# LoRA and low-rank residual kernel: half of z made as z^T for two tiles at once

## What is computed

```python
base   = x @ W.T                                      # W: 1024 x 1024
logits = x @ Wr.T + 5.0 * one_hot(itok)               # 8 experts
gates  = softmax over the two largest logits, 0 for the other six
h      = x @ A[e].T for each expert e                 # rank 16 each, 128 columns in all
cond   = base + 2.0 * sum_e gates[e] * h[e] @ B[e].T
out    = x + ((cond @ V) * S) @ U.T                   # V: 1024 x 256, U: 1024 x 256
```

## Time and profile before

| | us |
|---|---|
| median of three runs (lowest, highest) | 156.6 (156.23, 157.12) |
| the profiled execution | 156.3 |
| its span | 154.5 |
| PE busy | 150.1 (97%) |
| VectorE busy | 102.7 (66%) |
| GpSimd busy | 69.9 (45%) |
| ScalarE busy | 65.6 (42%) |
| granted TensorE clock, mean | 1.00 of full speed |

### The profile page before, as it was taken

One profiled execution on the slowest core, in us unless ns is written; L12 is line 12 of the kernel. 1 busy time (PEld: TensorE's weight loads), 2 busy tenths in 40 slices (PEclk: granted clock), 3 DMA queues, 4 the chain that ended last, 5 costly groups with the idle time before them and its releaser, 6 DMA issues.

```text
span 154.5 us, 2555 instructions
## 1 busy us (share of the span) xinstructions
PE 150.1 (97%) x883; PEld 139.9 (91%) x883; DVE 102.7 (66%) x299; ACT 65.6 (42%) x147; POOL 69.9 (45%) x53
## 2 busy tenths in 40 slices
PE   7999999999999999999999999999999999999991
PEld 5899999999988999989998999899999989998880
DVE  0887882942757898684669386929692967386862
ACT  4867772639615532551165125414431642233200
POOL 2000500259556650359355926591669068701800
PEclk9999999999999999999999999999999999999999
DMA  5999999994312064346338645764680087006184
GB/s 176 387 405 406 398 414 408 407 407 154 127 39 97 20 256 136 128 140 275 140 135 305 241 136 208 236 239 136 271 258 18 0 296 249 2 22 251 70 329 148
DMA packets 10669, 32.72 MB, mean 212 GB/s; under 512 B 1440, under 2 KB 1952, under 8 KB 10528
## 3 DMA queue, kind: packets, MB, share of 16 engines
q1 hardware_dynamic: 10368, 31.96, 55.7%
q10 hardware_dynamic: 288, 0.59, 1.0%
HBM read 24.16 MB, written 8.39 MB: 211 GB/s over the span
## 4 chain that ended last, share of the span: by engine, by line
PE 94%; DMA 3%; DVE 1%; ACT 0%; SPq 0%; issue 0%; DVEq 0%
PE pj L322 16%; PE pj L324 16%; PE pj L323 16%; PE fin L322 14%; PE fin L324 13%; PE fin L323 13%; DMA w_raw<-in_W 3%; PE zt L392 2%; PE gt L374 1%; PE zt L322 1%; PE zt L324 1%; PE zt L323 1%; DVE w_lo L704 0%; ACT w_hi L561 0%; DVE x_all L833 0%; SPq L217 0%
## 5 line engine op out<-in xcount | busy, mean ns | idle before, releaser
L278 POOL TENSOR_TENSOR xT_lo<-xt_raw,xT_hi 128x1024 fp32r<-128x1024 f32 x16 | 40.3, 2520 | 54.9 <-ACT xT_hi L576 54.9
L322 PE MATMUL pj<-proj_hi,xT_hi 128*128 128x392 f32 x128 | 45.0, 352 | 0.0
L324 PE MATMUL pj<-proj_hi,xT_lo 128*128 128x392 f32 x128 | 43.6, 341 | 0.0
L323 PE MATMUL pj<-proj_lo,xT_hi 128*128 128x392 f32 x128 | 43.5, 340 | 0.0
L293 POOL TENSOR_TENSOR x_all<-x_all,vw_raw 128x512 f32<-128x512 f32 x18 | 23.0, 1294 | 17.6 <-DVE vw_raw L808 17.6
L322 PE MATMUL fin<-v_hi,w_hi 128*128 128x256 f32 (+1 forms) x84 | 26.9, 320 | 0.1
L324 PE MATMUL fin<-v_hi,w_lo 128*128 128x256 f32 (+1 forms) x84 | 26.4, 314 | 0.0
L323 PE MATMUL fin<-v_lo,w_hi 128*128 128x256 f32 (+1 forms) x84 | 26.4, 314 | 0.0
L322 PEld LDWEIGHTS pj<-proj_hi,xT_hi 128*128 128x128 f32 x128 | 24.1, 188 | 1.0
L323 PEld LDWEIGHTS pj<-proj_lo,xT_hi 128*128 128x128 f32 x128 | 24.1, 188 | 0.5
L324 PEld LDWEIGHTS pj<-proj_hi,xT_lo 128*128 128x128 f32 x128 | 24.0, 188 | 0.0
(11 more groups left out here) (87 smaller groups left out, 230.6 us busy)
## 6 DMA issues: line engine op xcount, KB each, us to landing
xt_raw<-in_xt SPq DMA_DIRECT2D x16, 512.0 KB, 4.0
x_all<-in_x SPq DMA_DIRECT2D x16, 512.0 KB, 5.2
out<-x_all SPq DMA_DIRECT2D x13, 512.0 KB, 3.1
vw_raw<-in_VW SPq DMA_DIRECT2D x6, 384.0 KB, 6.7
w_raw<-in_W SPq DMA_DIRECT2D x8, 256.0 KB, 5.8
out<-x_all SPq DMA_DIRECT2D x5, 256.0 KB, 2.1
u_raw<-in_U SPq DMA_DIRECT2D x1, 1024.0 KB, 14.1
aw_raw<-in_AW SPq DMA_DIRECT2D x1, 544.0 KB, 6.8
```

The costliest lines, as they stand in the source:

```text
L278: nc.gpsimd.tensor_sub(xT_lo[:, t % 2, :, :], xt_raw[:, t % XTR, :, :], xT_hi[:, t % 2, :, :].bitcast(F32)).then_inc(xt_lo, 1)
L322: nc.tensor.matmul(dst, l_hi, r_hi, start=first, stop=False, skip_group_check=shared)
L323: nc.tensor.matmul(dst, l_hi, r_lo, start=False, stop=False, skip_group_check=shared)
L324: return nc.tensor.matmul(dst, l_lo, r_hi, start=False, stop=last, skip_group_check=shared)
```

## The change

The last 128 columns of z are no longer projected with the tile. `project` takes 264 columns (h, logits and the first half of z). `half_t` makes the second half for a pair, as z^T at once: `proj`'s last 128 columns are the stationary operand, x^T of two tiles (256 columns) the moving one. It needs x^T of both tiles, so the rings of split x^T hold four. The first half is copied (`copy_z`, now before the LoRA part is in it) and transposed once a tile, inside `half_t`. `transpose_gh` and `mix` work on a pair: `mix` adds the LoRA part to z^T, with B^T V stationary. `zt` is now ordered by half and tile (`zt_v`), and B^T V moves to the bank `gt`. `b_raw` and `u_raw` share memory with `w_raw`, so that their loads wait until the first 4 and 12 half chunks of W are split.

All lists are written by pair. PE's is: project the even tile, `second_part` of two pairs back, project the odd tile, `first_part` of the pair before, gh transposes, `half_t`, `mix`.

```diff
-        xT_hi = sb("xT_hi", [P, 2, DC, P], F32R)
+        xT_hi = sb("xT_hi", [P, XTR, DC, P], F32R)
...
# SP
                 if k == 6:
-                    sp.dma_start(b_raw[:, :, :], B).then_inc(b_load, 16)
-            load_xt(1)
+                    sp.wait_ge(w_lo_done, 4)
+                    sp.dma_start(b_raw, B).then_inc(b_load, 16)
+            for t in range(1, XTR):
+                load_xt(t)
             sp.dma_start(s_col[:, :], S).then_inc(s_load, 16)
-            sp.dma_start(u_raw[:, :, :], U).then_inc(u_load, 16)
-            for t in range(2, XTR):
-                load_xt(t)
+            sp.wait_ge(w_lo_done, 12)
+            sp.dma_start(u_raw, U).then_inc(u_load, 16)
             for t in range(XR):
                 load_x(t)
...
+            for p in range(PAIRS):
+                if 2 * p >= XR:
+                    load_x(2 * p)
+                    load_x(2 * p + 1)
+                if 2 * p + XTR < TILES:
+                    load_xt(2 * p + XTR)
+                    load_xt(2 * p + 1 + XTR)
+                if p == 2:
+                    store_head(0)
+                    store_head(1)
+                if p >= 3:
+                    store_pair(p - 2)
...
# GpSimd
             split_x(0)
             split_x(1)
             split_x(2)
+            pool.wait_ge(gh_done, 2)
+            split_x(3)
             pool.wait_ge(y_done, 2)
-            make_tsum(0)
-            make_tsum(1)
-            split_x(3)
-            pool.wait_ge(gh_done, 3)
-            make_tsum(2)
-            make_tsum(3)
...
+            for j in range(4):
+                make_tsum(j)
+            for p in range(1, PAIRS):
+                if p < PAIRS - 1:
+                    pool.wait_ge(gh_done, 2 * p + 2)
+                    split_x(2 * p + 2)
+                    split_x(2 * p + 3)
+                if p >= 2:
+                    pool.wait_ge(fin_read, READS * (p - 2) + 1)
+                    side(2 * p - 1, 0, 1)
+                    side(2 * p - 2, 1, 1)
+                    pool.wait_ge(fin_read, READS * (p - 2) + 3)
+                    side(2 * p - 1, 1, 2)
...
# TensorE
+            def project(t):
+                q, r = t % 2, t % XTR
+                pe.wait_ge(xt_lo, t + 1)
+                if t >= 2:
+                    pe.wait_ge(gh_done, t - 1)
+                    pe.wait_ge(z_copied, t - 1)
+                for k in range(DC):
...
+                    last = triple(pj[q][:, 0:TCOLS], xT_hi[:, r, k, :], xT_lo[:, r, k, :],
+                                  proj_hi[:, k, 0:TCOLS], proj_lo[:, k, 0:TCOLS], k == 0, k == DC - 1)
+                    if t == 2 and k == MH:
+                        mix(0)
+                last.then_inc(pj_done, 1)
+
+            def half_t(p):
+                r = (2 * p) % XTR
+                dst = zt_v[:, 1, :, :]
+                for k in range(DC):
+                    last = triple(dst, proj_hi[:, k, TCOLS:COLS], proj_lo[:, k, TCOLS:COLS],
+                                  xT_hi[:, r:r + 2, k, :], xT_lo[:, r:r + 2, k, :], k == 0, False, shared=True)
+                    if k == 2:
+                        pe.wait_ge(z_copied, 2 * p + 2)
+                        for t in range(2):
+                            nc.tensor.matmul(zt_v[:, 0, t, :], z_sb[:, t, :], ident[:, :], start=False, stop=False,
+                                             is_transpose=True, skip_group_check=True)
+                last.then_inc(xt_used, 1)
...
+            def mix(p):
+                if p == 0:
+                    pe.wait_ge(bv_lo_done, 1)
+                pe.wait_ge(gt_lo, p + 1)
                 for m in range(MC):
+                    cols = slice(m * P, (m + 1) * P)
+                    last = triple(zt[:, 2 * m * P:2 * (m + 1) * P], bv_hi[:, cols], bv_lo[:, cols],
+                                  ghT_hi[:, :], ghT_lo[:, :], False, True, shared=True)
                 last.then_inc(zt_done, 1)
...
+            project(0)
+            make_bv()
+            project(1)
+            half_t(0)
+            transpose_gh(0)
+            for p in range(1, PAIRS):
+                project(2 * p)
+                if p >= 3:
+                    second_part(p - 2)
+                project(2 * p + 1)
+                if p == 1:
+                    pe.wait_ge(us_lo_done, MC)
+                    pe.wait_ge(za_lo, 1)
+                    expand(0, bank_a, 0, 0, BANK)
+                    expand(0, bank_b, 0, BANK, D)
+                    pe.wait_ge(zb_lo, 1)
+                    expand(0, bank_c, MC, 0, BANK)
+                    expand(0, bank_d, MC, BANK, D)
+                else:
+                    first_part(p - 1)
+                transpose_gh(p)
+                zt_free(p)
+                half_t(p)
+                mix(p)
...
# ScalarE
+            def pair(p):
+                split_za(p - 1)
+                if p == 1:
                     split_zb_plain(0)
+                else:
+                    copy_x22(p - 1)
+                    split_zb(p - 1)
+                copy_z(2 * p)
+                exp_top(2 * p)
+                if p < PAIRS - 1:
+                    split_x(2 * p + 2)
+                if p == 1:
                     split_t(0)
+                copy_z(2 * p + 1)
+                exp_top(2 * p + 1)
+                if p >= 2:
+                    copy_u(p - 1)
+                if p < PAIRS - 1:
+                    split_x(2 * p + 3)
+                if p == 1:
                     split_t(1)
+                split_gh(p)
...
+                if i == OC + 6:
+                    split_x(1)
             for b in range(FINS):
                 split_p(b)
-            split_x(1)
+            copy_z(0)
             exp_top(0)
             split_x(2)
+            act.wait_ge(bv_done, 1)
+            nc.scalar.activation(bv_hi[:, :], bv_ps, ACT.Copy, scale=SCALING).then_inc(bv_hi_done, 1)
             act.wait_ge(s_load, 16)
             act.wait_ge(u_load, 16)
-            for m in range(MC):
-                make_y(m)
+            make_y(0)
+            copy_z(1)
+            exp_top(1)
+            make_y(1)
+            split_x(3)
...
             split_gh(0)
             split_us(0)
             split_us(1)
...
# VectorE
+            def pair(p):
+                split_za(p - 1)
+                if p == 1:
+                    split_zb_plain(0)
+                    split_us(0)
+                    split_us(1)
+                else:
+                    sums(p - 1)
+                    split_zb(p - 1)
+                if p >= 3:
+                    xb0(p - 2)
+                    xa1(p - 2)
+                gates_top(2 * p)
+                gates_apply(2 * p)
+                gates_top(2 * p + 1)
+                gates_apply(2 * p + 1)
+                if p == 1:
                     residual_end(0, bank_a, 0, 0, BANK)
                     residual_end(1, bank_b, 0, BANK, D)
                     split_t(0)
                     residual_end(2, bank_c, 1, 0, BANK)
+                    residual_end(3, bank_d, 1, BANK, D)
+                    split_gh(p)
                     split_t(1)
                 else:
+                    up(p - 1, 1)
+                    up(p - 1, 2)
+                    xb1(p - 1)
+                    xa0(p - 1)
+                    split_gh(p)
...
+            dve.wait_ge(b_hi_done, 1)
+            nc.vector.tensor_sub(b_lo[:, :, :], b_raw, b_hi[:, :, :].bitcast(F32)).then_inc(b_lo_done, 1)
             for b in range(FINS):
                 split_p(b)
-            dve.wait_ge(b_hi_done, 1)
-            nc.vector.tensor_sub(b_lo[:, :, :], b_raw[:, :, :], b_hi[:, :, :].bitcast(F32)).then_inc(b_lo_done, 1)
             dve.wait_ge(setup, 2)
             gates_top(0)
             gates_apply(0)
...
```

More of the change, by code:

```diff
@@ L33, in adaln_ffn @@
     COLS = ER + E + RANK
+    TCOLS = ER + E + P
     MH = HQ // P
@@ L92, in adaln_ffn @@
         gate = sb("gate", [P, E], F32)
[L93 to L96, removed]
+        gh = sb("gh", [P, 2, ER], F32)
+        ghT_hi = sb("ghT_hi", [P, 2 * P], F32R)
+        ghT_lo = sb("ghT_lo", [P, 2 * P], F32R)
+        z_sb = sb("z_sb", [P, 2, P], F32)
         zs = sb("zs", [P, 5, P], F32)
@@ L365, in p_chunk @@
                     last.then_inc(w_used, 1)
[L367 to L379, removed]
@@ L385, in transpose_z, with zt_free @@
+            def zt_free(p):
+                if p >= 1:
                     pe.wait_ge(za_lo, p)
-                if p == 1 and t % 2 == 1:
+                if p == 1:
                     pe.wait_ge(zb_lo, 1)
@@ L468, in make_bv @@
                 last.then_inc(bv_done, 1)
[L470 to L476, removed]
-                    if s == 0 and k % 2 == 0:
-                        pe.wait_ge(p_lo, k // 2 + 1)
-                    last = project(s, k)
-                    if s >= 1 and k == gh_at:
-                        transpose_gh(s - 1)
-                    if s >= 1 and k == mix_at and k < DC - 1:
-                        if s == 1:
```

(61 more changed lines are left out.)

166 lines of the change are left out of this document (48 added, 118 removed).

## The result

| | before | after |
|---|---|---|
| median (lowest to highest), us | 156.86 (156.23 to 157.44) | 158.44 (158.14 to 158.91) |
| profiled execution, its span | 156.3, 154.5 | 158.57, 156.8 |
| first projection to last matmul starts | 28.15 to 150.91 = 122.76 | 29.38 to 153.16 = 123.78 |

The direction was forecast, the size was not: I had said 160.9 us, 4.0 to 4.6 us slower, and it is 1.6 to 2.3. The wide range of 156.9 to 163.5 holds the time, but the forecast's own 159.0 to 162.5, to which I had given 0.60, does not.

The account below looks back on a forecast made before the run. TensorE's own instructions were taken to bound the kernel (busy 150.1 of 154.5 us). 156.3 + 0.4 (PE's work) + 0.3 (start) + 2.2 (us_lo) + 1.7 (ghT_lo) = 160.9 us; forecast 159.0 to 162.5, wide range 156.9 to 163.5.

Parts of the forecast that it names:

- PE's own work: TensorE's matmuls per pair: 264 columns taken at 0.125 us each, so +0.05 a pair, +0.4 us for eight.
- rival B: Faster: head covered and 264 columns at the pace of 256, -1.5 us, 154.8 us; chance 0.06.
- a sign that it is wrong: From pair 3 on, a pair period over 15.2 or under 14.6 us would show the forecast wrong.
- Start: Up to the first projection: split_x(1) holds the port, w_lo, b_lo and first p_lo come later, +0.3 us.
- us_lo: Pair 1, before the first expansion: PE waits for VectorE's us_lo, which takes turns with GpSimd's tsums, +2.2 us.
- ghT_lo of pair 1: Before mix(1): PE waits for ghT_lo, behind residuals and split_t(0), which meets GpSimd's split_x(4), +1.7 us.
- Rival A: Head covered: VectorE's chain in pair 1 runs within PE's work, its 3.9 us go, 157.0 us; chance 0.16.
- Later pairs: After pair 1: every wait has 0.6 us or more of slack, so 14.8 us a pair, as before.
- rival C: A wait in every pair: late gates on VectorE, 0.5 us in each of five pairs, 163.4 us; chance 0.12.
- D: A late load: u, behind x^T and under six x loads, 2 us late gives 162.9 us; chance 0.06.

Follow-up runs that it names:

- gh_early: Changed kernel with ghT of pair 1 split ahead of t and of two residuals, on VectorE and ScalarE, no wait changed: 1.011 of before (1.007 to 1.015).
- experiment 2: Changed kernel with one added wait: GpSimd starts its four tsums only once us_lo is whole; 159.37 us, 1.019 of before (1.016 to 1.022).
- after_again: The changed kernel measured once more on another occasion, no edit: 1.016 of before (1.013 to 1.019), median 158.77 us.
- experiment 1: The kernel before and the changed kernel each run once more without edit: 1.000 (0.998 to 1.002) and 1.016 (1.013 to 1.019) of before.
- experiment 5: Changed kernel with ghT of pair 1 split early, the head's lists reordered on ScalarE, VectorE and GpSimd, b_lo behind split_p: 154.75 us, 0.988 of before.

## Why the prediction was right and wrong

**PE's own work: the step that failed.** I had bounded 264 columns between 0.120 and 0.125 and took the upper end, on the ground that 392 lies above the line through 256 and 512 because it ends in 8 odd columns. It measures 0.1208, and the widths show that the odd columns are not the reason: 264 ends in the same 8 as 392 and lies over 2 ns below the line through 256 and 512, while 384 ends in none and lies 1 ns above it. The curve bends below 288. With 0.1208, 48 x (0.1208 - 0.1792) + 2.88 - 0.23 = -0.15 a pair; the pair measured -0.19. The term was +0.4 and is -1.5 us. It was rival B's pace. The period of 14.57 us also lies under the 14.6 that the prediction had named as a sign that it is wrong. The Trainium skill's figure for an isolated matmul (TensorE: Matmul & The Clock Gate, "Wait — 56ns, not 53.3ns?") gave a small gain, so it had the sign right; but no width of these runs agrees with N/2.4 plus 2.5 ns (136 columns: 59 by it as an estimate, 105 measured; 512: 216 and 228).

**Start: the mechanism right.** +0.3 was said. GpSimd, VectorE and PE in `gh_early`, the trace with the longest wait there:

```profile
24.23 2.40 POOL L285 TENSOR_TENSOR xT_lo<-xt_raw,xT_hi 128x1024 fp32r<-128x1024 f32 x1 [4.32 <-ACT xT_hi L578]
...
24.70 2.48 DVE L705 TENSOR_TENSOR w_lo<-w_raw,w_hi 128x512 fp32r<-128x512 f32 x1 [1.30 <-ACT w_hi L563]
27.11 1.21 DVE L881 TENSOR_TENSOR b_lo<-w_raw,b_hi 128x1024 fp32r<-128x1024 f32 x1
28.24 2.47 DVE L714 TENSOR_TENSOR proj_lo<-fin,proj_hi 128x512 fp32r<-128x512 f32 x4
...
29.06 0.36 PE L326 MATMUL pj<-proj_hi,xT_hi 128*128 128x264 f32 x1
```

split_x(1) holds w_lo of chunk 15, b_lo follows, and PE waits for p_lo. The wait is nothing in the first trace, where the matmuls ahead were late themselves, and 0.15 to 0.29 in four others. It is gone in the three kernels that have b_lo behind `split_p` again.

**us_lo: right.** 2.2 said, 1.98 measured, by the same turns at the port, which experiment 2 shows by taking one side away. The prediction's reading, that the first to ask keeps the port for one instruction and the other engine comes next, holds here: 4.11 us for two subtractions of 1.2.

**ghT_lo of pair 1: mechanism right, size twice too large.** 1.7 said, 0.84 measured. Gh of tile 3 ended at 54.35, not 54.8, since ScalarE gave exp earlier than I had it; the chain behind it was 0.2 shorter; and PE came for it 0.3 us later, at 58.7. Rival A, that the head is covered, falls.

**The clock: not in the prediction at all.** These terms give 156.3 - 1.5 + 0.3 + 2.0 + 0.8 = 157.9. In `after_again`'s trace, where the clock falls behind the gap, the expansions take 1.6 us more and the 0.8 before mix(1) is hidden behind them: 158.7, and its median is 158.77. The first median, 158.44, is not explained by the clock: three of its four executions had it whole and took 158.14 to 158.57. In the one with a trace (158.57) the first projection was 0.9 us later than forecast, for the late loads of experiment 1; of the other two there is no trace.

**Later pairs: right on the waits.** Neither trace of the changed kernel has a new gap there; rival C falls. So does D: nothing waited for u.

So a loss was forecast for the right reasons, and its size was wrong because a gain of 1.5 us was booked as a cost of 0.4 and, second, because the wait before mix(1) was put 0.9 too high. The time stayed inside the wide range by its lower bound, which belonged to rival A, a kernel without the two gaps; that is luck, not foresight.

## What to carry to other kernels

Where a change trades few wide instructions for more narrow ones, the pace of the new width is the forecast: measure it, or take both ends into the likeliest value, and don't draw a line through widths that lie further out. When work of a two-engine port is reordered, list every operation with both inputs in SBUF that stands beside it, the tiny ones too: in experiment 2 three of 8 or 16 elements each waited for one whole instruction of the other engine. And repair a head by order rather than by a wait: the wait of experiment 2 took away 1.8 us of the first gap and added 2.9 us behind it, the new order of experiment 5 removed both gaps and brought the gain of the change to light.

## What the runs showed of the hardware that I had not expected

- A gap of 2.0 us on PE, in otherwise dense work, was followed in 19 of 39 executions by a lower mean clock (0.989 or less). In the two of them with a trace it was half clock (matmuls of 512 columns 0.43 apart instead of 0.23), starting 1.5 us after PE had taken up work again and lasting some 3.3 us: 1.5 us on top of the gap's own length.
- A VectorE operation of 16 elements took 1.2 us instead of 0.15 to 0.18 while GpSimd's tsums ran.
- Projection matmuls of 136 to 224 columns, each with its weight load, started 0.105 to 0.110 us apart: 88 columns more cost 5 ns.
